# A hint for the loop's closing branch at the head of each batch iteration, on all five engines

## What is computed

```python
xn = _layernorm(x, axis=-1)
s = _L0_attn_ref(xn, ...)          # 16 heads, cumulative sums along the tokens
g = _silu(_L0_ffn_ref(xn, ...))    # 8 experts, two loops of routing
x = x + s * g
xn = _layernorm(x, axis=-1)
s = _L1_attn_ref(xn, ...)          # 16 heads of 8, softmax over all 1024 tokens
g = _silu(_L1_ffn_ref(xn, ...))    # 2 layers of windowed attention and a gated FFN
x = x + s * g
return x
```

## Time and profile before

| | us |
|---|---|
| median of 3 runs | 2710.52 |
| lowest and highest run | 2709.03, 2713.8 |
| span of the profiled execution, first to last instruction | 2703.9 |
| median of the runs less that span (start and end of a launch) | 6.6 |
| PE busy | 2181.8 |
| DVE busy | 2004.4 |
| ACT busy | 1437.2 |
| POOL busy | 583.7 |

### The profile page before, as it was taken

The page is one execution under the profiler, slowest core; times in us unless marked ns, Lnnn a source line. Parts: engine busy times, 40 slices in busy tenths (PEclk is TensorE's granted clock), DMA queues, the critical chain, the costliest instruction groups (busy, mean ns, idle before and its releaser), DMA issues.

```text
span 2703.9 us, 46770 instructions
## 1 busy us (share of the span) xinstructions
PE 2181.8 (81%) x17520; PEld 1245.8 (46%) x17520; DVE 2004.4 (74%) x4188; ACT 1437.2 (53%) x2637; POOL 583.7 (22%) x400
## 2 busy tenths in 40 slices
PE   3799589877879959978679977987877995888867
PEld 3567322364647612246455741235564772223646
DVE  4775799678675589867777469967877657997677
ACT  1334278674633438756643425767473342775745
POOL 0062100214043200040406310012312530003040
PEclk9999799989979969989888988998987996999889
DMA  4000200101000020010100021001100003001010
GB/s 149 0 1 1 76 22 9 25 14 30 13 10 1 22 62 18 10 30 5 30 21 1 1 70 26 10 13 24 26 11 17 1 1 83 18 10 30 5 30 20
DMA packets 58920, 63.92 MB, mean 24 GB/s; under 512 B 17136, under 2 KB 44080, under 8 KB 58160
## 3 DMA queue, kind: packets, MB, share of 16 engines
q1 hardware_dynamic: 55480, 57.77, 8.5%
q10 hardware_dynamic: 3192, 2.90, 0.3%
HBM read 25.19 MB, written 15.01 MB: 15 GB/s over the span
## 4 chain that ended last, share of the span: by engine, by line
PE 47%; DVE 29%; ACT 13%; issue 6%; DMA 2%; SPq 2%; POOL 0%; DVEq 0%; ACTq 0%; POOLq 0%
PE PS L1338 44%; DVE arena L1095 10%; ACT arena L705 7%; DVE arena L1193 2%; ACT arena L648 2%; PE PS L1663 1%; DVE s_at L1168 1%; DVE arena L1198 1%; DVE arena L1161 1%; PE PS L1356 1%; DMA tmp<-xf 1%; DVE tmp L1168 1%; DVE arena L1279 1%; SPq L319 1%; ACT tmp L659 1%
## 5 line engine op out<-in xcount | busy, mean ns | idle before, releaser
L1338 PE MATMUL PS<-arena 128*32 128x256 f32 (+4 forms) x10240 | 802.1, 347 | 133.2 <-DVE arena L1095 52.9
L1095 DVE TENSOR_REDUCE arena<-PS 128x1 f32<-128x512 f32 x1024 | 640.2, 687 | 36.3 <-PE PS L1338 36.3
L648 ACT ACTIVATE arena<-PS 128x1024 f32<-128x1024 f32 x512 | 518.0, 1031 | 168.1 <-PE PS L1338 167.1
L1338 PEld LDWEIGHTS PS<-arena 128*32 128x32 f32 (+4 forms) x10240 | 310.6, 122 | 620.3 <-DVE arena L1095 263.5
L600 ACT ACTIVATE arena<-PS 128x512 f32<-128x512 f32 x256 | 150.9, 598 | 244.5 <-PE PS L1338 244.3
L1338 PEld LDWEIGHTS PS<-w2e,arena 128*128 128x128 f32 x2048 | 246.0, 192 | 50.3 <-issue 49.7
L1338 PE MATMUL PS<-w2e,arena 128*128 128x128 f32 x2048 | 247.6, 275 | 0.2
L1058 DVE TENSOR_TENSOR arena<-PS,arena 128x512 f32<-128x512 f32 x128 | 86.3, 689 | 211.5 <-PE PS L1338 211.1
L705 ACT ACTIVATE arena<-PS,arena 128x128 f32<-128x128 f32 x512 | 230.5, 539 | 22.3 <-DVE arena L1229 20.1
L1338 PE MATMUL PS<-wqkv,arena 128*128 128x512 f32 x384 | 185.7, 625 | 24.9 <-ACT arena L687 21.7
L455 POOL TENSOR_TENSOR zz<-zz,arena 128x512 f32<-128x512 f32 x104 | 135.4, 1302 | 268.2 <-DVE arena L1058 239.5
(11 more groups left out here) (300 smaller groups left out, 3485.5 us busy)
## 6 DMA issues: line engine op xcount, KB each, us to landing
arena<-arena SPq DMA_DIRECT2D x120, 128.0 KB, 2.3
scr_q<-arena SPq DMA_DIRECT2D x40, 128.0 KB, 2.4
scr_k<-arena SPq DMA_DIRECT2D x40, 128.0 KB, 2.4
arena<-scr_k SPq DMA_DIRECT2D x24, 200.0 KB
arena<-scr_q SPq DMA_DIRECT2D x24, 192.0 KB
x_in<-in_x SPq DMA_DIRECT2D x5, 512.0 KB, 4.0
out_x<-tmp SPq DMA_DIRECT2D x4, 512.0 KB, 3.8
wqkv<-in_wqkv SPq DMA_DIRECT2D x1, 1536.0 KB, 7.3
```

Source lines behind the costliest of these rows:

```text
L648: act.activation(pb[:, n % 8], pair(2 * (n % 2)), ACT.Exp).then_inc(S["p"], 1)
L1095: dve.tensor_reduce(mxp[:, h % 2, j, t, hf:hf + 1], PS[:, ring_bank("mx", h, n), :], AX, ALU.max)\
L1338: return pe.matmul(o, w, v, start=start, stop=stop, **kw)
```

## The change

The five loops are opened through the general form of the loop, with `hint_back_edge=True`. The loop itself stays as it was: same counter, same add, same branch, same body. In front of the body's first instruction stands now one more instruction on each engine, a branch prefetch hint. [...] It is executed once in each pass, four times on each engine. Nothing else is added, removed or moved.

```diff
-            with sp.Fori(0, B) as b:
+            with nc.Fori(0, B, engines=(sp.engine,), hint_back_edge=True) as b:
...
-            with pool.Fori(0, B) as b:
+            with nc.Fori(0, B, engines=(pool.engine,), hint_back_edge=True) as b:
...
-            with act.Fori(0, B) as b:
+            with nc.Fori(0, B, engines=(act.engine,), hint_back_edge=True) as b:
...
-            with dve.Fori(0, B) as b:
+            with nc.Fori(0, B, engines=(dve.engine,), hint_back_edge=True) as b:
...
-            with pe.Fori(0, B) as b:
+            with nc.Fori(0, B, engines=(pe.engine,), hint_back_edge=True) as b:
```

## The result

The changed kernel takes 2700.51 us, the median of 16 runs (2694.78 to 2714.26), against 2710.29 us (2705.07 to 2725.29, also 16 runs) for the kernel before on the same chip. The ratio is 0.9961 with an interval of 0.9946 to 0.9977. On 2710.29 us that is 10.6 us less, between 6.2 and 14.6. The two medians alone differ by 9.8 us.

The account below looks back on a forecast made before the run. PE is busy 81% of the span, but the prediction aimed at 14.62 us of "issue" waits at three batch passages: -13.15 + 0.3 = -12.85 us, so 2710.5 - 12.9 = 2697.6 us, range 2694.0 to 2703.5.

Parts of the forecast that it names:

- The three stalls: At the three batch passages, "issue" pieces of 14.62 us shrink by 13.15 us; hints on PE's path add 0.3 us.
- PE, DVE and ACT behave as POOL does now: At each batch passage, these engines return soon after their branch, leaving 0.5 us on the chain in place of 4.82.
- The hint, 0.1 us: At the loop's head, each hint costs 0.1 us, three times on PE's path; the first pass is free.
- 2.6 us of fetch and 2 us of queue: At the branches of PE, DVE and ACT, the stall is a 2.6 us plain fetch plus 2 us queueing behind the output.
- What is late next: After the restart, ACT's 1.28 us table load ends some 0.1 us after PE's fourth transpose, but costs nothing.
- The clock, 0: At the batch passages, PE's clock still falls despite the shorter gap; effect 0, with 1.5 us kept each side in sum.
- The end, 0: After the last pass, the wrong hint costs 0 in the span; 2.6 us on SP kept for the upper end.
- Everything inside the batches keeps its length to 1 us or so: A sign in the changed profile: work between the batch passages keeps its length to 1 us or so.
- What lies around the span: Outside the profiled span: the runs' median lies 6.6 us above it, and the edit does not touch that.
- The idle hint: Rival, chance 0.11: the hint does nothing, or PE, DVE or ACT stays unhelped at the passages; 2710.8 us.
- Half of the stall: Rival, chance 0.06: at the three edges 2.6 us of fetch goes, 2 us of queueing stays; 7.8 us saved, 2703 us.
- The slower case: Rival, chance 0.04: the hint displaces the next block's fetch, 2.6 us each pass, and the branch stall stays; 2720.9 us.

Follow-up runs that it names:

- hint_three: The changed kernel with hints on PE, ACT and DVE only, SP's and POOL's loops as before; 2698.61 us, ratio 0.9953 to the kernel before.
- hint_pe: The kernel before with a hint on PE's loop only; 2714.42 us, ratio 1.0013.
- hint_late: The kernel before with the same hints on all five engines, but at the end of each loop body; 2712.71 us, ratio 0.9991.
- wait_head: The kernel before with one already satisfied wait, no hint, at the loop's head on SP, ACT, DVE and PE; 2710.12 us, ratio 1.0001.
- go_first: The changed kernel with SP's five clears and `go` moved ahead of the wait for `obuf` and the output's issue; 2705.27 us, ratio 0.997.
- a_again: The changed kernel once more, unchanged, with a second profile; 2698.8 us, ratio 0.9962 to the kernel before.
- b_again: The kernel before once more, unchanged, for a second profile; 2709.61 us in one run.
- out_late: The kernel before, no hint, with the 512 KB output transfer issued only after SP's 82 clears; 2723.9 us, ratio 1.0035.
- pe_alone: The kernel before with the output transfer issued after SP's clears, and hints on ACT and DVE only; 2715.16 us in one run.

## Why the prediction was right

The forecast was 2697.6 us with a range of 2694.0 to 2703.5; 2700.51 us came. The case was the likeliest one, and its mechanism is shown by both sides: three hints give all of it (hint_three), one gives none (hint_pe), and a hint in the wrong place gives none (hint_late). The measured time is 2.9 us above the forecast. 0.7 us of that is the edge (next item); the rest lies in the length of the passes, which no term forecast, so the closeness of the total is in part luck.

- *The three stalls, -13.15 us plus 0.3.* Measured on the chain: -12.13 against the -12.85 of the sum. The step that was mis-sized is "PE, DVE and ACT behave as POOL does now", 0.5 us left plus 0.1 for the hint. A hinted head costs PE 0.48 us for the branch and lets DVE start after 0.6, where POOL, hinted or not, takes 0.2 to 0.3. So 0.81 to 0.86 us are left per edge instead of 0.6, in sum 0.7 us more.
- *The hint, 0.1 us.* Right. It lasts 36 ns on PE, and the next instruction starts 0.1 us after it. In the first pass there is room for it: in the kernel before PE is at its loop at 102.1 us and its first transpose starts at 109.51. Another instruction in its place costs nothing that the timed runs show, within 0.2% (wait_head).
- *2.6 us of fetch and 2 us of queue.* Wrong in its parts, though no term of the sum stood on it. With empty queues PE still needs 3.4 to 3.9 us, DVE and ACT 2.9 to 3.3. The queue is about 1 us.
- *What is late next.* The table load costs nothing, as said. ACT's first copy now starts right behind it, at 756.19. PE's eight transposes begin at 755.03 and take 1.98 us, and the second copy starts at 757.03, after waiting for them as before.
- *The clock, 0.* Right at the first edge, in kind and nearly in length. The windows of the changed kernel (length, then busy time of PE, PEld, DVE, ACT and POOL, then the granted clock):

```profile
750.70:754.20 3.50, 0.00 (x0) 0.00 (x0) 2.48 (x4) 0.56 (x1) 0.00 (x0) 0.50 0.00 0
755.00:764.20 9.20, 8.50 (x34) 7.42 (x35) 7.65 (x46) 4.03 (x6) 0.00 (x0) 0.50 0.13 42
764.40:767.00 2.60, 2.24 (x15) 1.17 (x13) 1.21 (x7) 0.96 (x2) 0.00 (x0) 1.00 0.00 0
```

  The clock is at 0.50 in the gap and back at 1.00 some 9.3 us after PE's restart; it was 8.8 us before. The shorter pause did not keep it up: it fell 0.8 us after PE's last matmul (749.81 to 750.63), where it had fallen after 0.9 us, and stayed down for 13.65 us, four steps of 3.41 us, where it had been five. At the other two edges the rise came 9.7 us after the restart, where it was 8.7 and 8.4. So the low stretch became one step shorter at the first edge. No run shows by itself what that is worth, nor the 1.5 us that the range kept for the clock in sum. What the runs show is a stretch some 220 us into a pass that takes some 5 us more at once when the granted clock over it is 0.74 instead of 0.86 (go_first), so the clock's share of the range was too small for single runs.
- *The end, 0.* Right for the span. SP's last branch lasts 64 ns against 48. The 3.7 us on POOL were not foreseen; they are hidden.
- *"Everything inside the batches keeps its length to 1 us or so."* Wrong as a statement on single profiles. The first pass grew by 1.65 us here, and in a_again another stretch did by 3.8. The kernel before varies in the same way without any hint (b_again), so the sum took no harm from it.
- *What lies around the span.* The prediction put 6.6 us between span and median. The profiled executions show 1.8 us (2696.49 and 2694.7). If the same holds for the kernel before, its profiled execution took about 2705.7 us, less than any of the three timed runs. Span and median went down together, so this did no harm.
- *The rivals.* The idle hint falls: the hint at the head works, though it is executed some 650 us ahead of its branch (102.6 and 754.3 us on PE in the first pass), and on PE, DVE and ACT it is the late one that does nothing. "Half of the stall" falls with 0.8 us left; PE takes 35 packets of 16 KB from 102 to 752.6 us in the kernel before, one in 18.6 us on average, so a block is long work for it, as the argument against this rival had it. The slower case asked for a stall of 2.6 us where an engine leaves its first block; the next 16 KB packet starts 2.4 us after PE's branch, and PE's first sixteen matmuls start as far behind its restart as before; the four stretches leave room for 2.9 us in sum, not for the 10.4 it priced. Without a hint PE, DVE and ACT stall at the taken branch for 4.2 to 4.8 us in the kernel before; with one at the loop's head one 16 KB packet per passage is gone, and 4.05 us of PE's first branch with it.

## What to carry to other kernels

Where a loop's body is so long that its head is fetched again (here the bodies of 294 to 2,944 instructions stalled, and the body of 172 did not, nor did it with 40 more), look at the loop's edge in the chain of waits for a piece of "issue" and at the instruction after each engine's branch; the stall is worth a hint only if every engine that the next pass needs first gets one. Put the hint at the head of the body: at the end of it, 1.8 to 5.7 us ahead of the branch, it did nothing for PE, ACT and DVE. The likely reason is that it must stand ahead of the block that holds the branch. Here about 0.8 us was left per edge out of 4.8, and the engines whose return is hidden gave nothing.

## What the hardware showed that was not expected

- Without a hint at the head of the loop the return took 2.4 to 3.1 us on SP, 3.4 to 3.9 on PE with empty queues (out_late, pe_alone), and 4.0 to 4.8 on PE, DVE and ACT behind a transfer of 512 KB that begins at the same time. With one it took 0.4 to 0.7 us on PE, DVE and ACT and 0.2 to 0.3 on SP. On POOL it took 0.2 to 0.3 us in every kernel.
- A hint did not start a fetch when it was executed (hint_late: no instruction packet for 5.7 us). It seems to take the place of a fetch that was made anyway (145 packets of 16 KB against 148), and on SP it did away with five packets of 8 KB per passage.
- A wrong hint cost nothing on four engines. POOL's end came up to 3.7 us late in some placements, and 0.9 us late in kernels with hints on other engines alone.
- The length of a pass varies with the granted clock in it, though not with that alone (the fourth body of b_again). Here is one kernel, the repeat of the changed one, at the same 6 us of its second and third stretches (240.4 us behind the start of each "issue" piece):

```profile
994.00:1000.00 6.00, 5.23 (x36) 0.99 (x36) 4.42 (x8) 2.27 (x3) 0.00 (x0) 0.54 0.00 0
1642.40:1648.40 6.00, 4.88 (x50) 1.33 (x50) 6.00 (x10) 3.38 (x4) 0.00 (x0) 1.00 0.01 3
```

  Both windows begin with the 1052nd matmul behind their "issue" piece. The same matmuls ran at 0.54 in one pass and at 1.00 in the next: 36 of them against 50 in the same time. The one stretch is 648.48 us, the other 645.12. A difference of 3 us between two single profiles of this kernel is therefore no evidence of a gain or a loss. The "issue" pieces repeat to 0.02 us in both kernels.
